# Graph layers on one core: VectorE and ScalarE copy a tile each for every fifth group of edges instead of every tenth, and read node numbers as two-byte integers

## The reference

```python
def _L0_gnn_ref(x, edge_attr, ...):
    row, col = (edge_index[0], edge_index[1])
    msg = _mlp(jnp.concatenate([x[row], edge_attr], axis=1), W1, b1, g1, be1)
    sums = jax.ops.segment_sum(msg, col, num_segments=N)
    agg = sums / jnp.maximum(cnt, 1.0)[:, None]
    return _mlp(jnp.concatenate([x, agg], axis=1), W2, b2, g2, be2)
def _L1_gnn_ref(x, edge_index, edge_attr, W, b, eps):
    msg = jax.nn.relu(x[src] + edge_attr)
    agg = jax.ops.segment_sum(msg, dst, num_segments=x.shape[0])
    h = (1.0 + eps) * x + agg
    return jax.nn.relu(h @ W.T + b)
x = _layernorm(x + _L0_gnn_ref(...), axis=-1)
x = _layernorm(x + _L1_gnn_ref(...), axis=-1)
```

## Time and profile before

| | |
|---|---|
| median of 3 runs | 8584.98 us (8583.19 to 8587.3) |
| the profiled execution | 8583.33 us, its span 8581.6 us |
| block C, first to last gather | 4720.38 to 8489.29 us of the span |
| gathers in block A, block C | 3125, 3001 |
| busy share PE, DVE, ACT, POOL | 63%, 33%, 25%, 69% |
| granted TensorE clock, mean | 0.59 of full speed |

### The profile page before, as it was taken

How to read it: one execution, slowest core, us unless ns; L and a number is a source line. 1 busy time by engine, 2 the same in 40 slices (tenths; PEclk the granted TensorE clock), 3 DMA queues, 4 the chain that set the end, 5 groups by cost and what they waited for, 6 DMA issues and landing times. The chain is left out here.

```text
span 8581.6 us, 117915 instructions
## 1 busy us (share of the span) xinstructions
PE 5392.4 (63%) x22956; PEld 3145.6 (37%) x22956; DVE 2870.3 (33%) x12804; ACT 2143.6 (25%) x9969; POOL 5878.9 (69%) x6150
## 2 busy tenths in 40 slices
PE   4555555555555555555995666666666666666666
PEld 2222222232222222224993333333333333333334
DVE  3222222222222222224885333333333333333334
ACT  0111111111111111112775333233333333333322
POOL 7777777777777777773001777777777777777774
PEclk6555555555555565556996555555555555555555
DMA  3333333333333333333772222222222222222221
GB/s 102 78 78 78 78 78 78 78 78 78 78 78 78 78 79 78 78 78 96 197 198 69 60 54 55 54 55 54 55 55 54 55 55 54 55 54 54 55 54 40
DMA packets 809867, 634.77 MB, mean 74 GB/s; under 512 B 546288, under 2 KB 629415, under 8 KB 808721
## 3 DMA queue, kind: packets, MB, share of 16 engines
q1 hardware_dynamic: 566454, 323.37, 14.4%
q0 software_dynamic: 196448, 204.48, 12.4%
q10 hardware_dynamic: 46450, 102.55, 4.0%
HBM read 520.99 MB, written 108.90 MB: 73 GB/s over the span
## 5 line engine op out<-in xcount | busy, mean ns | idle before, releaser
L387 POOL DMA_INDIRECT Z<-in_x_dram,src_idx x3125 | 2986.6, 956 | 971.2 <-issue 950.9
L1215 POOL DMA_INDIRECT X<-x_scratch,src_idx x3001 | 2855.1, 951 | 939.7 <-issue 899.8
L421 PE MATMUL PS<-ident,Z 128*128 128x128 f32 x3125 | 747.1, 398 | 1686.2 <-DMA Z<-in_x_dram,src_idx 1678.0
L1232 PE MATMUL PS<-X,ident 128*128 128x320 f32 x1126 | 763.3, 779 | 1289.9 <-DMA X<-x_scratch,src_idx 1289.9
L432 PE MATMUL PS<-ZT,W_sb 128*64 128x320 f32 x2500 | 1461.6, 740 | 0.0
L472 ACT ACTIVATE ZT<-PS 128x640 f32<-128x640 f32 x625 | 440.0, 704 | 3502.1 <-PE PS L421 3502.1
L538 DVE BATCH_NORM_STATS2 stats<-PS 128x320 f32 (+1 forms) x624 | 279.5, 490 | 3038.8 <-remote 3015.2
L421 PEld LDWEIGHTS PS<-ident,Z 128*128 128x128 f32 x3125 | 527.2, 202 | 2016.1 <-issue 1738.6
L1324 DVE COPY rows_by_dve<-table 64x1 f32 x7936 | 999.8, 146 | 619.9 <-issue 619.9
L1288 ACT ACTIVATE rows_by_act<-table 64x1 f32 x7936 | 893.4, 199 | 420.2 <-issue 420.2
L1232 PEld LDWEIGHTS PS<-X,ident 128*128 128x128 f32 x1126 | 267.6, 296 | 1806.5 <-DMA X<-x_scratch,src_idx 1806.4
(11 more groups left out here) (143 smaller groups left out, 3312.4 us busy)
## 6 DMA issues: line engine op xcount, KB each, us to landing
Z<-in_edge_attr_dram SPq DMA_DIRECT2D x625, 160.0 KB, 3.3
E<-in_edge_attr_dram SPq DMA_DIRECT2D x625, 160.0 KB
h_scratch<-h_ring ACTq DMA_DIRECT2D x312, 320.0 KB
hT<-h_scratch SPq DMA_DIRECT2D x312, 320.0 KB
Z<-in_x_dram,src_idx POOLq DMA_INDIRECT x3125, 2.5
X<-x_scratch,src_idx POOLq DMA_INDIRECT x3001, 2.5
x_nodes<-in_x_dram SPq DMA_DIRECT2D x1, 3125.0 KB
x_ring<-in_x_dram SPq DMA_DIRECT2D x25, 125.0 KB
```

The costliest lines, as they stand in the source:

```text
L387: nc.gpsimd.indirect_dma_start(out=Z[:, r, j, 0:D], out_offset=None, in_=x, in_offset=bass.IndirectOffsetOnAxis(ap=src_idx[:, n:n + 1], ax ...
L421: last = nc.tensor.transpose(banks(2 * (s % 2), 2, P, EG)[:, j * P:(j + 1) * P], Z[:, r, j, :], ident[:, :])
L1215: nc.gpsimd.indirect_dma_start(out=X[:, r, j, :], out_offset=None, in_=x1_dram, in_offset=bass.IndirectOffsetOnAxis(ap=src_idx[:, n:n + 1] ...
L1232: nc.tensor.matmul(PS[:, s % SUMS, 0:HC], ident[:, :], X_r, start=False, stop=True).then_inc(sum_put, 1)
```

## The change

`COPIED` becomes every fifth group (9, 14, 19, ...: 124 groups, where 62 were). With 4 such groups in a body, 4 rows of numbers are kept for each of the two tiles, and `copied_src` is filled by 8 transfers, where 4 were. The numbers are then cast once, at the beginning of block C, to two-byte integers on VectorE (`copied_node`); ScalarE waits for that cast before its first slot. A step is now 32 copies behind one load of 32 registers, in slots 0 to 3 of each 5. The wait for `src_copied` moves from each step to the cast.

```diff
-        EVERY = 2 * S
+        EVERY = S
+        PERIODS = BODY // EVERY
         COPIED_SLOT = EVERY + 4
-        STEP = 16
-        copied_src = sb(ctx, "copied_src", [4, 31, P], int32)
+        STEP = 32
+        copied_src = sb(ctx, "copied_src", [2 * PERIODS, BODIES, P], int32)
...
                     for j, row in ((BY_DVE, 0), (BY_ACT, 1)):
-                        for T in range(2):
-                            of = src.rearrange("(g p j) -> j g p", p=P, j=TG)[j, COPIED[T]::2 * EVERY, :]
-                            sp.dma_start(copied_src[2 * row + T:2 * row + T + 1, :, :], of.unsqueeze(0),
+                        for T in range(PERIODS):
+                            of = src.rearrange("(g p j) -> j g p", p=P, j=TG)[j, COPIED[T]::BODY, :]
+                            sp.dma_start(copied_src[PERIODS * row + T:PERIODS * row + T + 1, :, :], of.unsqueeze(0),
                                          allow_slow_non_contiguous=True).then_inc(src_copied, 16)
...
+            copied_node = sb(here, "copied_node", [2 * PERIODS, BODIES, P], mybir.dt.int16)
+            nodes_ready = sem("nodes_ready")
...
-            def copy_rows(engine, regs, row, k, s, copy, to, copied):
+            def copy_rows(engine, kind, row, k, s, copy, to, copied):
                 T = s // EVERY
-                engine.wait_ge(src_copied, 64)
                 step = s % EVERY
-                engine.load(regs, copied_src[2 * row + T:2 * row + T + 1, ds(at(k, 1, 0), 1), step * STEP:(step + 1) * STEP]
-                            .rearrange("o a n -> o (a n)"))
-                for n in range(STEP):
-                    node = engine.snap(regs[n], min_val=0, max_val=NODES - 1)
+                row = PERIODS * row + T
+                _, nodes = nc.values_load_multi_w_load_instructions(
+                    copied_node[row:row + 1, ds(at(k, 1, 0), 1), step * STEP:(step + 1) * STEP].rearrange("o a n -> o (a n)"),
+                    [kind], min_val=0, max_val=NODES - 1, skip_runtime_bounds_check_because="src holds numbers of nodes")
+                for n, node in enumerate(nodes):
                     last = copy(to[:, T % 2, step * STEP + n:step * STEP + n + 1], table[0:D, ds(node, 1)])
...
                         if not by_engine(k, s):
-                            each = 32 if r == COPIED_SLOT % RING else 0
-                            pe.wait_ge(gathered[r], at(k, 32 * TG - 2 * each, (16 * TG - each) * (s // RING) + 16 * TG))
+                            pe.wait_ge(gathered[r], at(k, 32 * TG, 16 * TG * (s // RING) + 16 * TG))
...
-                        pe.wait_ge(gathered[r], at(k, 2 * 48, 48 * (s // RING) + 16 * TG))
+                        pe.wait_ge(gathered[r], at(k, 2 * 48, 48 * (s // RING) + (48 if r == COPIED_SLOT else 16 * TG)))
...
+                    act.wait_ge(nodes_ready, 1)
...
+                    dve.wait_ge(src_copied, 16 * 2 * PERIODS)
+                    nc.vector.tensor_copy(copied_node[:, :, :], copied_src[:, :, :]).then_inc(nodes_ready, 1)
+                    dve.wait_ge(nodes_ready, 1)
```

More of the change, by code:

```diff
@@ L174, in gnn_kernel @@
         idx_flat = idx_ring[:, :, :].rearrange("p s j -> p (s j)")
-        EVERY = 2 * S
+        EVERY = S
+        PERIODS = BODY // EVERY
         COPIED_SLOT = EVERY + 4
         BY_DVE, BY_ACT = 4, 3
-        STEP = 16
-        copied_src = sb(ctx, "copied_src", [4, 31, P], int32)
+        STEP = 32
+        copied_src = sb(ctx, "copied_src", [2 * PERIODS, BODIES, P], int32)
         src_copied = ctx.enter_context(nc.semaphore("src_copied"))
         COPIED = [g for g in range(COPIED_SLOT, G, EVERY)]
-        dve_rows = [nc.vector.alloc_register(f"dve_row{n}") for n in range(STEP)]
-        act_rows = [nc.scalar.alloc_register(f"act_row{n}") for n in range(STEP)]
         window_regs = [nc.vector.alloc_register(f"window_reg{s}") for s in range(S)]
@@ L1168, in copied_count @@
             def copied_count(k, s):
-                return at(k, 2, (s - COPIED_SLOT % EVERY) // EVERY)
-            def copy_rows(engine, regs, row, k, s, copy, to, copied):
+                return at(k, PERIODS, (s - COPIED_SLOT % EVERY) // EVERY)
+            def copy_rows(engine, kind, row, k, s, copy, to, copied):
                 T = s // EVERY
-                engine.wait_ge(src_copied, 64)
                 step = s % EVERY
-                engine.load(regs, copied_src[2 * row + T:2 * row + T + 1, ds(at(k, 1, 0), 1), step * STEP:(step + 1) * STEP]
-                            .rearrange("o a n -> o (a n)"))
-                for n in range(STEP):
-                    node = engine.snap(regs[n], min_val=0, max_val=NODES - 1)
+                row = PERIODS * row + T
[3 more added lines that the diff above has]
+                for n, node in enumerate(nodes):
                     last = copy(to[:, T % 2, step * STEP + n:step * STEP + n + 1], table[0:D, ds(node, 1)])
@@ L1284, in body @@
                             if slots == BODY and s % EVERY < P // STEP:
-                                copy_rows(act, act_rows, 1, k, s, by_act, rows_act, act_copied)
+                                copy_rows(act, mybir.EngineType.Activation, 1, k, s, by_act, rows_act, act_copied)
                     def by_act(to, of):
@@ L1320, in body @@
                             if slots == BODY and s % EVERY < P // STEP:
-                                copy_rows(dve, dve_rows, 0, k, s, by_dve, rows_dve, dve_copied)
+                                copy_rows(dve, mybir.EngineType.DVE, 0, k, s, by_dve, rows_dve, dve_copied)
                     def by_dve(to, of):
```

## The result

| | before | after |
|---|---|---|
| median of 4 runs each, same chip | 8584.08 us | 10904.13 us |
| span of the profiled execution | 8581.6 | 10900.7 |
| first `hT` consumer of block B | 4017.97 | 4112.83 |
| first gather of block C | 4720.38 | 4815.09 |
| last add of VectorE in block C | 8497.72 | 10817.01 |

The ratio is 1.2702 (95% interval 1.2684 to 1.272). 8527 us had been predicted, with a range from 8495 to 8620. The first part follows the prediction: block B's first work comes 94.9 us later, where 96 had been put down, and everything up to the first gather of block C keeps that distance. Block C, from first gather to last add, goes from 3777 to 6002 us, 2225 more, where 156 fewer had been expected.

A forecast was written before the change was run, and what follows sets the result against it. GpSimd's gather issue was taken to bound block C: 8583.3 - 155.7 for gathers + 96 for transfers + 2 for the cast = 8525.6, with 1.7 to the median 8527 us; range 8495 to 8620.

The forecast's parts named there:

- What bounds block C, and the value of fewer gathers: Block C: GpSimd's issuing sets the pace, 1.256 us a gather; 124 fewer gathers save 155.7 us.
- The loads of 32 registers: VectorE in block C: 32 two-byte numbers cost nothing more than 16 four-byte ones; bounds nothing or 0.73 us more per load.
- the prediction's own sum: VectorE per body of block C: 72.3 us plus copies 32.3, breaks 1.3 and remains 2, sum 107.9 of 115.5 us.
- VectorE becomes the bound: Rival, block C: loads cost by register, VectorE's body 119.6 us, 4.1 over GpSimd's, kernel 8654 us; chance 0.11.
- The rule of the Trainium skill: Register loads: about 200 ns per register, so 51 us more a body and over 1300 us slower; set aside by the trace.
- VectorE's other load: Block C, per body: 256 more copies at 0.126 us, 32.3 us, and four more instruction-stream breaks, 1.3 us.
- The 2 us set aside for remains: VectorE per body: idle time between matrix and add that counts as waiting when late, a third of 6.4 us.
- Deadlines, ScalarE, PE: Block C: copied rows ready before PE comes; ScalarE 80 of 115.5 us per body, PE 79 plus a few; none the bound.
- The cast: Before VectorE's first slot of block C: 2 to 5 us, hidden in idle time; may hold GpSimd once, 2 us put down.
- Eight transfers for four: End of block A: four more transfers drain one after another with nothing hiding them, 4 x 24 = 96 us more.
- Holds of GpSimd: Rival, block C: one-hot matrices delay gathers more often, up to 8648 us; chance of a shift over 40 us 0.05.
- the stronger form: Skill rule: fp32 SBUF copies on VectorE lock GpSimd out, eating the gain; trace held to disagree for one-column copies.

The follow-up runs named there:

- e1: The changed kernel with node numbers kept as four-byte integers, not two-byte: 8534.47 us against 8608.07 for the kernel before on that chip, ratio 0.9915.
- e0_loads: The kernel before with twelve extra VectorE loads that the built program left out, so the same but for a cast of 64 numbers: 8607.47 us beside 8608.07.
- e6: The changed kernel with four-byte numbers and 248 small transfers spread over block A instead of eight at its end: 8407.63 against 8587.73 us, ratio 0.9788.
- e0b_loads: The kernel before with twelve extra VectorE register loads ahead of its first slot of block C, their registers used by copies: 8584.91 us beside 8587.73.
- e2: The changed kernel with two loads of 16 two-byte numbers for each one of 32: 10997.51 us beside 8608.07 for the kernel before.

## Why the prediction was wrong

*What bounds block C, and the value of fewer gathers*: right. In e1 a gather follows each 1.258 us, where the kernel before on that chip (e0_loads) has 1.262, and with the drains out of the way (e6) 124 fewer of them are worth what 124 x 1.256 says and 7 us more.

*The loads of 32 registers*: **the step that failed.** "I take nothing more, as the row of the same 64 bytes is nearest." Its two bounds, 0 and 0.73 us more per load, came from three loads that all fetch four-byte numbers, none of them begun 4 bytes off. From them one sees a price by piece of 16 bytes, which was read correctly, but none of them could tell whether it holds for another type. It doesn't: 6.0 us more per load instead of 0. By the prediction's own sum that is 107.9 + 16 x 6.0 = 204 us a body; 192.4 were measured, so the sum without the loads was some 12 too high. The rival that stood nearest (VectorE becomes the bound) had the mechanism, but its price of 4.1 us per body was 76.9.

The rule of the Trainium skill that the prediction weighed (Runtime: NRT & Kernel Launch, "Instruction fetch mechanics", about 200 ns per register) was set aside on the strength of the cheap four-byte loads. The page states it for loads from HBM; these come from SBUF. The changed kernel's trace agrees with it for two-byte numbers (220 ns each), and e0b_loads does for four-byte ones begun 4 bytes off (226 ns); it disagrees for the other four-byte ones, 66 to 69 ns a number when 16 or 32 come at a time. The rule should have had a chance of its own; with 32 x 0.2 = 6.4 us a load, an estimate from the page's figure, it comes near the 7.11. The prediction priced by it only the 16 registers that were added, 3.2 us and over 1300 us in all. Priced for the whole load, 6.4 in place of 1.10, the same sum gives 107.9 + 16 x 5.3 = 192.7 us a body and 31 x 77.2 = 2393 us, beside the 2384 of the trace; that this estimate is so near is partly luck, as the page's 0.2 is below the measured 0.22 and the 107.9 was too high.

*VectorE's other load*: the step that was mis-sized besides. 107.9 us were put down with loads of 1.10 us, so 123.9 with 2.10, and e1 takes 110, 14 less. About 5 of them are the copies: in a row of 32 one more takes (3.71 - 0.146) / 31 = 0.115 us, not 0.126. For the rest the waits of the kernel before in 5000 to 8000 us go beside those of e1 above:

```profile
DVE rows_by_dve L1324 <- issue: 500.2, 474, 1.5
...
DVE hot_c L1301 <- issue: 162.9, 99, 4.1
```

Per body the time in front of the copies grows from 20.1 to 34.3 us, 14.2 where 16 for the loads and 1.3 for breaks make 17.3. In front of the one-hot matrices, where the loop's turn and the loads of window starts lie, it falls from 6.5 to 2.6 us: it had been counted as work, and more than half of it goes away when the engine is late. The 2 us set aside for remains are counted as waits. That makes the 14 within half a us. The gap in front of a step's copies in the changed kernel, 6.93 to 7.03 us, is also a little shorter than its load of 7.11, while before it was longer, 1.17 against 1.10; what overlaps there no run shows.

This error was not harmless: with 123.9 us the sum would have put e1 31 x 8.4 = 260 us over the forecast. That e1 comes out near it is owed to a sum that was 14 too high, and the point from which a dearer load costs anything lies above the 1.0 us more of e1, not at 0.47.

*Deadlines, ScalarE, PE*: right as far as e1 shows them; PE has no wait for `rows_by_dve` in its trace. (The "eight slots" of before are the slots in which copies are made; the last of them is slot 7, and PE wanted the rows behind `segment_sum` of slot 10, three slots later against two now. No term hangs on it.) *The cast*: right in size. It took 2.21 us and held one gather for 2.4:

```profile
4826.48 3.31 POOL L1216 DMA_INDIRECT X<-x_scratch,src_idx  x1 [0.30 <-issue]
...
4827.46 2.21 DVE L1334 CAST copied_node<-copied_src 8x3968 int16<-8x3968 int32 x1
```

*Eight transfers for four*: right, 94.9 us in the changed kernel (96 predicted). SP's issues in its timeline answer to the earlier trace rows, ScalarE's first work to the earlier trace rows:

```profile
3909.69 176.99 SPq L374 DMA_DIRECT2D copied_src<-in_src_dram  x8
4088.19 31.97 SPq L620 DMA_DIRECT2D hT<-h_scratch  x10
```

```profile
4088.20 1.28 ACT L632 ACT_TABLE_LOAD   x1 [89.74 <-PEq L123]
...
4112.83 1.94 ACT L632 ACTIVATE mT<-hT,shift_col,scale_col 128x640 f32<-128x640 f32 x2 [23.35 <-DMA hT<-h_scratch]
```

The barrier comes at 4088 (4087 predicted): ScalarE and VectorE stand there 89 us, until SP's issues return. *Holds of GpSimd*: the mean gather of block C is 948 ns in the changed kernel and 953 in e1, against 951 before and 957 on e1's chip, so the stronger form in which copies lock GpSimd out is not seen for one-column copies; it is for the wide cast above.

## What to carry to other kernels

A price read from a trace holds for the form it was read from. Where a change alters an operand's type or its address, and many cheap operations stand behind it, the new form has to be measured by itself, or a rule that says otherwise has to keep a chance and reach into the range. Count what an engine needs per period against the engine that sets the pace, and look at both: dear loads for every tenth group were free, and for every fifth they cost 27%. Transfers of many single numbers ahead of a barrier cost their draining time, even when the issuing engine has nothing else to do; spread over a stage that has time they cost nothing that e6 shows.

## What the runs showed of the hardware that was not expected

- A register load on VectorE of four-byte numbers side by side in SBUF, begun at the tile's beginning or a multiple of 32 bytes from it, takes 0.25 us more for each further 16 bytes (0.35 us for 4 numbers, 0.60 for 8, 1.10 for 16, 2.11 for 32). Two-byte numbers, or four-byte numbers begun 4 bytes off, take 0.22 us each (3.59 and 3.62 us for 16). On ScalarE the changed kernel's loads of 32 take 6.88 us and e1's 1.97.
- A transfer of 3968 single four-byte numbers takes 24 to 28 us, about 6 ns a number, and holds the issue of the next one on its queue for that long.
- A cast on 8 partitions by 3968 numbers on VectorE (2.21 us) held a GpSimd gather for 2.4 us (3.31 instead of 0.94). With the same cast or a copy of that size in e1, e2 and e6 one gather takes 2.56 to 3.29 us.
